# Gate sums from high and low halves, and routing and second normalisation in places of their own

## The reference, cut to what matters

```python
g = k                                              # the gate is the key projection
gl = jax.nn.log_sigmoid(g.astype(jnp.float32)) / GATE_NORM       # 16.0
def step(S, inp):
    q_t, k_t, v_t, g_t = inp                       # softmax(q), softmax(k), v, gl
    S = S * jnp.exp(g_t)[..., None] + k_t[..., None] * v_t[..., None, :]
    o_t = jnp.einsum('bhk,bhkv->bhv', q_t, S)
    return (S, o_t)
o = 0.5 * y + 0.5 * o_gla                          # y: the causal softmax attention
x = _layernorm(x + o @ Wo)
top_w, top_idx = jax.lax.top_k(routing_weights, TOP_K)           # 2 of 8
y = jnp.einsum('etf,efd->etd', jax.nn.silu(g) * u, w_down)
x = _layernorm(x + jnp.einsum('te,etd->td', comb, y))
```

## Time and profile before

| | us |
|---|---|
| median of 3 runs | 981.12 |
| profiled execution | 980.99 |
| its span | 979.2 |
| TensorE busy | 928.0 (95%) |
| ScalarE busy | 661.8 (68%) |
| VectorE busy | 654.4 (67%) |
| GpSimd busy | 636.1 (65%) |

### The profile page before, as it was taken

The page is one execution under the profiler, slowest core; times in us unless marked ns, Lnnn a source line. Parts: engine busy times, 40 slices in busy tenths (PEclk is TensorE's granted clock), DMA queues, the critical chain, the costliest instruction groups (busy, mean ns, idle before and its releaser), DMA issues.

```text
span 979.2 us, 18417 instructions
## 1 busy us (share of the span) xinstructions
PE 928.0 (95%) x5347; PEld 718.5 (73%) x5347; DVE 654.4 (67%) x1597; ACT 661.8 (68%) x2139; POOL 636.1 (65%) x609
## 2 busy tenths in 40 slices
PE   7899999999999999999999999999999989989990
PEld 4678777778787878787887877878777766766770
DVE  4777776767676767677676869676887664431274
ACT  6677777777777777777677776777667664543453
POOL 6878675767565657676767667766658881553342
PEclk9999999999999999999999999999999999997995
DMA  7101100000000000900000000010102121332364
GB/s 250 34 17 33 39 1 2 6 12 6 1 0 0 0 1 10 257 6 2 1 1 1 1 7 6 24 39 3 61 1 79 38 85 45 92 107 84 98 180 133
DMA packets 34050, 43.20 MB, mean 44 GB/s; under 512 B 3756, under 2 KB 27950, under 8 KB 33840
## 3 DMA queue, kind: packets, MB, share of 16 engines
q1 hardware_dynamic: 30224, 33.76, 11.8%
q0 software_dynamic: 3744, 8.43, 2.4%
HBM read 25.58 MB, written 18.43 MB: 45 GB/s over the span
## 4 chain that ended last, share of the span: by engine, by line
PE 85%; DVE 4%; ACT 4%; issue 3%; POOL 2%; another core or an unknown queue 1%; DMA 0%; POOLq 0%; DVEq 0%; ACTq 0%
PE OA L590 14%; PE PR L473 12%; PE S L543 11%; PE MS L563 9%; PE S L572 7%; PE S L689 5%; PE OA L552 5%; PE OA L583 4%; PE OA L706 4%; PE PR L519 3%; PE PR L513 3%; PE S L534 1%; PE MS L502 1%; ACT eqk L821 1%; PE MS L594 1%
## 5 line engine op out<-in xcount | busy, mean ns | idle before, releaser
L1496 POOL TENSOR_TENSOR qd<-eqk,eg 128x512 f32<-128x512 f32 x63 | 75.9, 1205 | 163.1 <-issue 157.2
L590 PE MATMUL OA<-wT,V 128*128 128x512 f32 x320 | 150.2, 600 | 0.2 <-DVE wT L1081 0.2
L783 ACT ACTIVATE S<-S,nm 128x128 f32<-128x128 f32 (+3 forms) x256 | 126.8, 495 | 26.8 <-DVE nm L998 22.8
L821 ACT ACTIVATE eqk<-qkv,nmx 128x128 f32<-128x128 f32 x320 | 124.4, 396 | 6.0 <-DVE nmx L1073 5.5
L998 DVE TENSOR_REDUCE nm<-S 128x2 f32<-128x256 f32 (+3 forms) x128 | 102.0, 817 | 29.1 <-PE S L543 23.4
L590 PEld LDWEIGHTS OA<-wT,V 128*128 128x128 f32 x320 | 60.2, 192 | 70.9 <-issue 70.4
L1484 POOL TENSOR_TENSOR eqk<-eqk,rse 128x640 f32<-128x640 f32 x63 | 79.7, 1265 | 49.9 <-DVE rse L1116 25.7
L1032 DVE TENSOR_TENSOR pr<-S,rl 128x256 f32<-128x256 f32 (+3 forms) x128 | 105.5, 824 | 5.0
L1473 POOL TENSOR_TENSOR rp<-qkv,cos 128x640 f32<-128x640 f32 x64 | 99.9, 1560 | 6.4 <-ACT qkv L811 4.9
L1476 POOL TENSOR_TENSOR rp<-rp,rt 128x640 f32<-128x640 f32 x64 | 99.5, 1554 | 5.0
L1473 POOL TENSOR_TENSOR rt<-qkv,sin 128x640 f32<-128x640 f32 x64 | 99.5, 1555 | 0.0
(11 more groups left out here) (173 smaller groups left out, 2506.1 us busy)
## 6 DMA issues: line engine op xcount, KB each, us to landing
qkv<-slot_x SPq DMA_DIRECT2D x46, 129.0 KB
pr<-plane SPq DMA_DIRECT2D x16, 256.0 KB, 3.1
gu_w<-in_wgu SPq DMA_DIRECT2D x8, 352.0 KB, 3.6
slot_x<-zero SPq DMA_DIRECT2D x2, 1290.0 KB, 9.8
stage<-in_wqkv SPq DMA_DIRECT2D x6, 384.0 KB, 3.4
xraw<-in_x_cols SPq DMA_DIRECT2D x16, 128.0 KB, 2.4
acc<-in_x_rows SPq DMA_DIRECT2D x1, 2048.0 KB, 11.1
dn_w<-in_wdn SPq DMA_DIRECT2D x8, 256.0 KB, 4.2
```

Of the source, the lines that this page charges most:

```text
L590: last = pe.matmul(OA[:, :], V[:, j, :], wT[:, j, :], start=(c == 0 and j == 0), stop=(j == c))
L783: nc.scalar.activation(S[:, h, 0:n], S[:, h, 0:n], ACT.Exp, bias=nm[:, h:h + 1], scale=1.0, accum_out=ls[:, h:h + 1]).then_inc(s_exp, 1)
L821: last = nc.scalar.activation(eqk[:, par, h * 128:(h + 1) * 128], qkv[:, c % C, h * 128:(h + 1) * 128], ACT.Exp, bias=nmx[:, h:h + 1], sca ...
```

## The change

1. **Sums from halves.** `gl` is cast by ScalarE to `gl_hi` (float32r, new `gates_high`), VectorE subtracts that from `gl` to `gl_lo` (new `gates_low`), and `gate_sums` adds products of both with the constants, of which a float32r copy `sums` is made once (ScalarE, at the start). exp(-|g|) is written over |g|.
2. **Order.** `gates_high(g, c + 1)` stands behind `o_out` at the head of ScalarE's step, `gates_low(g, c + 1)` behind `update_state` and ahead of both `score_max` on VectorE.
3. **Routing.** compare of block 2 from mid 21 to late 20; slots from mid 24 and mid 25 to late 23 and late 24; tile_experts(0) from late 23 to late 26.
4. **Spread writes.** Tiles by step: 25: 0, 1; 26: 2, 3; 27: 4, 5, 6; 28: none; 29: 7, 8; 30: 9, 10, 11. In the experts' loop one indirect DMA a slot tile at q = 15 to 22, in place of two at q = 14 to 17.
5. **Own statistics columns.** mv, ve, rstd and the shift of the second normalisation have a column for each of the 16 tiles, so `moments2` no longer waits for ScalarE. The combining starts one slot tile sooner, ScalarE normalises one tile a slot tile from q = 40 on, the last tile is normalised by VectorE, and the stores go in six parts, the first ahead of the last four row loads.

```diff
-        gmat = cm[:, 256:384]
-        halves = cm[:, 384:386]
+        gmat = cm[:, 256:386]
+        gl_hi = sb("gl_hi", [P128, D], F32R)
+        gl_lo = sb("gl_lo", [P128, D], F32R)
+        sums = sb("sums", [P128, P128 + 2], F32R)
-        COMPARE_AT = {("late", 9): 0, ("late", 13): 1, ("mid", 21): 2}
+        COMPARE_AT = {("late", 9): 0, ("late", 13): 1, ("late", 20): 2}
-        SLOTS_AT = {("mid", 24): 0, ("mid", 25): 1}
-        SEND_AT = {25: (0, 2), 26: (2, 4), 27: (4, 6), 28: (6, 8), 29: (8, 10), 30: (10, 12)}
+        SLOTS_AT, EXPERTS_AT = {("late", 23): 0, ("late", 24): 1}, ("late", 26)
+        SEND_AT = {25: (0, 2), 26: (2, 4), 27: (4, 7), 29: (7, 9), 30: (9, 12)}
...
-                pe.wait_ge(s_gl, u + 1)
+                pe.wait_ge(s_gll, u + 1)
...
-                pe.matmul(MS[:, 0:128], gmat, gl[:, :], start=True, stop=True)
-                pe.matmul(MS[:, 128:130], gl[:, :], halves, start=True, stop=True).then_inc(s_g, 1)
+                for i, part_ in enumerate((gl_hi, gl_lo)):
+                    pe.matmul(MS[:, 0:128], sums[:, 0:128], part_[:, :], start=(i == 0), stop=(i == 1))
+                for i, part_ in enumerate((gl_hi, gl_lo)):
+                    last = pe.matmul(MS[:, 128:130], part_[:, :], sums[:, 128:130], start=(i == 0), stop=(i == 1))
+                last.then_inc(s_g, 1)
...
+            def gates_high(g, c):
+                u = C * g + c
+                act.wait_ge(s_gl, u + 1)
+                later(act, s_g, u)
+                nc.scalar.copy(gl_hi[:, :], gl[:, :]).then_inc(s_glh, 1)
...
                     o_out(g - 1 if c == 0 else g, C - 1 if c == 0 else c - 1)
+                if n1:
+                    gates_high(g, c + 1)
                 if c:
                     carry_state(g, c)
...
             copy_out(0, 0)
             gate_logs(0, 0)
+            act.wait_ge(s_cst, 64)
+            nc.scalar.copy(sums[:, :], gmat).then_inc(s_sums, 1)
             features(0, 0)
+            gates_high(0, 0)
...
+            def gates_low(g, c):
+                u = C * g + c
+                dve.wait_ge(s_glh, u + 1)
+                later(dve, s_g, u)
+                nc.vector.tensor_tensor(gl_lo[:, :], gl[:, :], gl_hi[:, :].bitcast(F32), ALU.subtract).then_inc(s_gll, 1)
...
                 if c:
                     update_state(g, c)
+                if n1:
+                    gates_low(g, c + 1)
                 score_max(g, c, 0)
...
-                i = slice(2 * h, 2 * h + 2)
+                i = slice(TPB * n + 2 * h, TPB * n + 2 * h + 2)
                 dve.wait_ge(s_bn[2], 2 * TPB * n + 4 * h + 2)
-                later(dve, s_xo, TPB * n - 2 + 2 * h)
...
-            later_tiles = {37 + t: t for t in range(3 * TPB)}
+            later_tiles = {36 + t: t for t in range(3 * TPB)}
...
+            a = acc[:, TILES - 1, BODY]
+            nc.vector.tensor_scalar(a, a, mv[2][:, TILES - 1, 0:1], rstd[2][:, TILES - 1:TILES], ALU.subtract, ALU.mult).then_inc(s_last, 1)
...
-            sends = {14: 12, 15: 13, 16: 14, 17: 15}
-            deviations = {36 + 2 * i: (i // 2, i % 2) for i in range(5)}
+            sends = {15 + i: (3 * TPB + i // 2, i % 2) for i in range(2 * TPB)}
+            deviations = {35 + 2 * i: (i // 2, i % 2) for i in range(5)}
```

More of the change, by code:

```diff
@@ L263, in layer_kernel @@
         s_mark, s_back, s_bf = sem("s_mark"), sem("s_back"), sem("s_bf")
+        s_last = sem("s_last")
         s_yg = [sem(f"s_yg{i}") for i in range(4)]
         s_us = sem("s_us")
+        s_sums, s_glh, s_gll = (sem(n) for n in ("s_sums", "s_glh", "s_gll"))
         s_c0, s_cb, s_nmr, s_xo, s_out = (sem(n) for n in ("s_c0", "s_cb", "s_nmr", "s_xo", "s_out"))
@@ L439, in _, with store @@
                 load_slots(q)
-                if q >= 38:
-                    load_rows(q - 38)
-            for t in range(NT - 38, TILES):
-                load_rows(t)
[L444 to L451, removed]
+                if q >= 37:
+                    load_rows(q - 37)
+            ov = out.rearrange("b (t p) n -> p (b t) n", p=P128)
+            def store(a, b):
+                sp.dma_start(ov[:, a:b, :], acc[:, a:b, BODY]).then_inc(s_out, 16)
+            for t in range(NT - 37, TILES):
+                if t == 3 * TPB:
+                    sp.wait_ge(s_xo, TPB)
+                    store(0, TPB)
+                load_rows(t)
+            for a, b in ((TPB, 2 * TPB), (2 * TPB, 3 * TPB), (3 * TPB, 3 * TPB + 2), (3 * TPB + 2, TILES - 1)):
+                sp.wait_ge(s_xo, b)
+                store(a, b)
+            sp.wait_ge(s_last, 1)
+            store(TILES - 1, TILES)
+            sp.wait_ge(s_out, 16 * 6)
         @block.tensor
@@ L715, in _ @@
             pe.wait_ge(s_cst, 64)
+            pe.wait_ge(s_sums, 1)
             gate_sums(0, 0)
@@ L917, in y_out, with norm2 @@
                 nc.scalar.copy(yo[:, q % YO, :], OA[:, 0:HID]).then_inc(s_yo, 1)
[L919 to L922, removed]
+            def norm2(t):
+                a = acc[:, t, BODY]
+                act.wait_ge(s_nmr, t // 2 + 1)
+                nc.scalar.activation(a, a, ACT.Identity, bias=nmr[:, t:t + 1], scale=rstd[2][:, t:t + 1]).then_inc(s_xo, 1)
             def wo_high(i):
@@ L973, in _ @@
                     router_exp(3)
-                if q in (42, 43):
-                    for i in ((0, 1) if q % 4 == 2 else (2, 3)):
-                        norm2(0, i)
-            for n in (1, 2, 3):
-                for i in range(TPB):
-                    norm2(n, i)
+                if q >= 40:
+                    norm2(q - 40)
+            for t in range(NT + 2 - 40, TILES - 1):
+                norm2(t)
         @block.vector
@@ L1214, in slot_bases @@
                 link(nc.vector.tensor_scalar(base128[:, :], base[:, :], float(P128), -1.0, ALU.mult, ALU.add))
-                if s == 0:
-                    tile_experts(s)
             def tile_experts(s):
@@ L1332, in beside @@
                     slots(0, SLOTS_AT[at, k])
+                if (at, k) == EXPERTS_AT:
+                    tile_experts(0)
             def multiply(q):
@@ L1391, in _ @@
             feature_sums(0, 0)
+            gates_low(0, 0)
             clamp_gates(0, 0)
@@ L1545, in step @@
                     for t in range(*SEND_AT[k]):
-                        send(t)
+                        for r in range(2):
+                            send(t, r)
             def norm1(t):
@@ L1555, in norm1, with send @@
                                         ALU.subtract, ALU.mult).then_inc(s_x1a, 1)
-            def send(t):
+            def send(t, r):
                 s = 0 if t < SETS[0][1] else 1
-                if t == SETS[s][0]:
+                if t == SETS[s][0] and r == 0:
                     pool.wait_ge(s_sl, s + 1)
@@ L1564, in send @@
                     pool.wait_ge(s_x1a, SETS[s][1])
-                for r in range(2):
-                    nc.gpsimd.indirect_dma_start(slot_x[s], bass.IndirectOffsetOnAxis(ap=sloti[:, r, t:t + 1], axis=0),
-                                                 acc[:, t, :], None).then_inc(s_sent[s], 16)
+                nc.gpsimd.indirect_dma_start(slot_x[s], bass.IndirectOffsetOnAxis(ap=sloti[:, r, t:t + 1], axis=0),
+                                             acc[:, t, :], None).then_inc(s_sent[s], 16)
             def send_back(q):
@@ L1576, in rs2 @@
             def rs2(n, h):
-                i = slice(2 * h, 2 * h + 2)
+                i = slice(TPB * n + 2 * h, TPB * n + 2 * h + 2)
                 pool.wait_ge(s_ve[2], 2 * n + h + 1)
-                nc.gpsimd.tensor_tensor(rstd[2][:, i], ve[2][:, i], neghalf[:, i], ALU.pow).then_inc(s_rs[2], 1)
+                nc.gpsimd.tensor_tensor(rstd[2][:, i], ve[2][:, i], neghalf[:, 0:2], ALU.pow).then_inc(s_rs[2], 1)
             for c in range(2):
@@ L1613, in _ @@
                 if q in sends:
-                    send(sends[q])
+                    send(*sends[q])
                 if q in deviations:
```

19 lines of the change are left out of this document (8 added, 11 removed).

## The result

The changed kernel took 999.34 us (median of 4 runs, 997.08 to 1002.74), beside 980.62 for the kernel before (4 runs): ratio 1.0193, 95% interval 1.0157 to 1.0229. The forecast was 996, range 982 to 1006. The time went where the forecast put most of it, in the steps c = 0 and c = 1 of every group; the gain that was credited to the shorter sums does not exist.

A forecast was written before the change was run, and what follows sets the result against it. TensorE was taken to bound the kernel, busy 95% of the span and holding 85% of the chain. Terms 17.5 + 3.3 + 3 - 5 - 4 = +14.8 us on 981.12 gave 996 us; own range 988 to 1003, with neighbours 982 to 1006.

The forecast's parts named there:

- The gate sums: TensorE's sums per unit: four single-pass products at 0.06 us replace the 0.34 us float32 pair, 0.10 saved.
- Rival (c): Gate sums: float32r products of few columns no shorter than float32; four take 0.56 us, 1003 us total; chance 0.12.
- c = 0: First step of each four-step group: GpSimd's instruction holds the subtraction, sums released late; +0.59 us, 0.20 without the hold.
- rival (b): First step of each group: GpSimd doesn't hold the subtraction, 0.39 us less a group, 991 us; chance 0.12.
- c = 1: Second step of each group: VectorE waits for ScalarE's cast, maxima and later work queue behind it; +0.67 us.
- c = 2: Third step of each group: the subtraction puts 0.20 us in front of VectorE's clamp; +0.20 us.
- c = 3: Fourth step of each group: subtraction fits VectorE's idle time, TensorE's saving not seen; 0.
- Groups 1 to 12: The 12 undisturbed groups of four steps: 1.46 us longer each, 17.5 us in all; ends 8.4 and 24.
- Start: Kernel start and group 0: matrix copy delays features, first decay 1.3 us later, 0.5 a step; +3.3 us.
- Routing, groups 13 to 15: Moved routing and spread writes in the last groups, halves included: +3 us, bounds -4 and +7.
- Experts: Experts' loop: one scatter a slot tile spreads the writes that go with a stall; -5 us, bounds 0 and -10.
- End: Kernel end: own columns remove VectorE's 2.40 us wait, last tile on VectorE, smaller last store; -4 us, bounds -2 and -5.

The follow-up runs named there:

- run 7: Kernel before with only the four single-pass float32r sum products, low half left out, no cast or subtraction: 979.31 us beside 978.9, ratio 1.0005.
- run 11: Changed kernel with GpSimd's rescaling in c = 0 made to wait until the subtraction is done: 988.79 us beside 970.9, ratio 1.0198.
- run 5: Changed kernel with the subtraction moved behind both maxima in c = 1 alone: 993.54 us beside 978.9, ratio 1.0163.
- run 12: Changed kernel with unit 1's subtraction ahead of VectorE's wait for the rows of acc at the start: 991.53 us, ratio 1.0220.
- run 10: Kernel before plus routing, columns, stores, paired last writes, tiles 4 to 14 normalised behind the experts' loop, attention writes respread: 965.17 us, ratio 0.9941.
- run 4: Changed kernel with both halves made by VectorE right behind the gate logarithms, ScalarE's cast gone: 1012.65 us, ratio 1.0350.
- runs 1 to 8: Follow-up kernels in two sets of four on two chips, where the kernel before took 978.4 and 978.9 us.
- runs 9 to 12: Third set of four follow-up kernels, on a third chip, where the kernel before took 970.9 us.

## Why the prediction was right, point by point

- **The gate sums** (0.34 down to 0.24 us a unit, "6.4 us over 64 units if nothing else moved"): wrong. The step that failed is the choice of 0.06 a product from the row of bf16 products of 128 columns. The chain has 0.085 each, 0.34 in all, and run 7 shows a saving of nothing. The bounds (0.22 to 0.48) held it. The fact that decides it, two instructions a float32 product, was in the text ahead of the prediction, and the prediction did not count with it. Rival (c) had that fact right, that the float32r products are no shorter than the float32 ones, and its price wrong: 0.56 us for the four where 0.34 were measured, so 1003 us does not follow from it. The estimate from the Trainium skill (TensorE: Matmul & The Clock Gate, "Back-to-back issue gap"), 0.02 us a unit, was nearer than my row: it goes by 0.081 us a product, and the chain here has 0.085.
- **c = 0** (+0.59, from a release 0.69 late less 0.10 saved): +0.70. The release was right, the 0.10 were not there. The split between hold and cast is shown by run 11: +0.28 to 0.41 without the hold outside the loop (forecast 0.20). That speaks against rival (b) too, by which GpSimd doesn't hold the subtraction: 0.69 us beside GpSimd's instruction, 0.29 without. In groups 4 to 6 c = 0 lost 0.97 to 1.0: TensorE began its sums 0.23 to 0.29 us after the subtraction's end there, 0.05 elsewhere. Why is open.
- **c = 1** (+0.67, the queue behind VectorE's wait): +0.60; run 5 shows 0.5 of it to be the queue.
- **c = 2** (+0.20) and **c = 3** (0): +0.21 and 0.00. No run takes the 0.20 of c = 2 apart.
- **Groups 1 to 12** (17.5 us): 19.5. Seven of the twelve groups lost 1.37 to 1.53 us beside the forecast 1.46, in part by luck: the 0.10 that c = 0 did not save and the 0.07 that c = 1 lost less cancel. The 2.0 missing are the groups of the hardware loop (4 to 6, 1.4 together) and group 11 (2.39 us, so 0.9), less 0.5 in group 12; neither the loop's part nor that of group 11 is explained.
- **Start** (+3.3): +4.6. The first two steps lost 2.1 and 3.2 us, where 0.5 each and 1.3 for the first decay were forecast, the third was 0.5 shorter. A part of it is a term that I hadn't named: unit 1's subtraction stands behind VectorE's wait for the rows of acc, TensorE idled 2.97 us for it (until 22.13), and its clock was at the lower level from 21.0 to 27.9 us. How much that costs run 12 could not show. The 4.6 lie inside my bounds only if the 0 to 4 are those of group 0's steps, with the 1.3 on top.
- **Routing, groups 13 to 15** (+3, the halves in it): +1.3. Step 28 +1.98 (forecast 2.0) and step 29 -3.38 (forecast -3.3) were as put; steps 21 (-1.3, forecast +0.6), 24 (0.0, forecast +1.4) and 25 (-0.6, forecast +0.9) were better, steps 22 (+1.6) and 30 (+2.1, forecast +0.4) worse.
- **Experts** (-5): -5.5, with stalls of 1.3 to 2.8 us left behind outputs 17, 20 and 23. **End** (-4): -1.7, the term most out of size: VectorE's wait of 2.40 us is gone, and the last write back follows the last expert output by 1.1 us instead of 3.1. But the last tile's chain behind it (write back, row load, two combinations, moments, GpSimd's power, store) is as long as it was, 19.2 us beside 19.0. In the stretch before, the loop's, the last slots became 2.43 us apart instead of 1.95, with ScalarE's normalisations between them (run 10). **Last attention stretch** (nothing): +2.0, a wait of 1.95 us of TensorE, 1.85 before, behind which the clock this time went to half for 3.4 us. The prediction put this stretch at nothing without a word on it.

The sum was +14.8 and the measured spans differ by 20.1: the terms that were off, start 1.3, groups 2.0, last stretch 2.0, end 2.3, less routing 1.7 and experts 0.5, make the difference of 5.3. That the measured time came within 3.3 us of the forecast is in part luck too: the routing's steps missed by up to 1.9 us either way and ended 1.7 better than forecast.

## What to carry to other kernels

A float32 product already is two instructions on TensorE: splitting it by hand into high and low halves against a rounded constant saved none of them here (operands of 128 and 2 columns), and added a cast and a subtraction on two engines that feed TensorE. Read the count behind a product in the profile before you price it. And where an operation that waits for another engine goes into an in-order queue, ask how long it waits and who stands behind it, and what it stands behind itself: moved behind the two maxima, the same subtraction gave 0.5 us a group in one step and cost 0.7 in the next.

## What was not expected of the hardware

- VectorE's cast with a single SBUF input was held by GpSimd's instruction in flight: 1.17 us instead of 0.23 (run 4).
- In the gate sums the weight loads follow each other by 0.11 us with float32 and with float32r operands alike, in the four bf16 mask products by 0.055 (run 7 and the kernel before).
- The stall of the experts' loop went with the chip as well as with the writes. On the chips of runs 1 to 8 the excess was 4.1 to 5.2 us with one write in each of eight slots running (five kernels) and 7.7 to 8.2 with two in each of four (two kernels); on that of runs 9 to 12 it was 0.0 with one in each of eight (two kernels). What differs is open; the mean time of a packet in the two queues was alike on all (0.10 and 0.06 us).
